# Score products of two maxima and two exponentials issued together out of four row strips, in the third attention of a two-layer adaLN transformer

## What is computed

```
q = q * cos + rotate_half(q) * sin
k = k * cos + rotate_half(k) * sin
scale = HEAD_DIM ** (-0.5)                      # HEAD_DIM = 8, 16 heads
attn = jnp.einsum('bhsd,bhtd->bhst', q, k) / scale
attn = jax.nn.softmax(attn, axis=-1)            # no mask
out = jnp.einsum('bhst,bhtd->bhsd', attn, v)
```

## Time and profile before

| | us |
|---|---|
| median of 3 runs | 2082.59 |
| lowest and highest of them | 2069.64, 2089.3 |
| the profiled execution, its own time | 2063.7 |
| its span, first to last instruction | 2061.9 |
| busy in the span: PE, VectorE, ScalarE, POOL | 1778.0, 1016.9, 724.5, 391.8 |

### The profile page before, as it was taken

How to read it: one execution, slowest core, us unless ns; L and a number is a source line. 1 busy time by engine, 2 the same in 40 slices (tenths; PEclk the granted TensorE clock), 3 DMA queues, 4 the chain that set the end, 5 groups by cost and what they waited for, 6 DMA issues and landing times.

```text
span 2061.9 us, 32743 instructions
## 1 busy us (share of the span) xinstructions
PE 1778.0 (86%) x10932; PEld 1140.9 (55%) x10932; DVE 1016.9 (49%) x2471; ACT 724.5 (35%) x1533; POOL 391.8 (19%) x614
## 2 busy tenths in 40 slices
PE   5899999799999989989799999689898989997480
PEld 2555555445555545555588888555555555554260
DVE  2445454244444443444588888555545555553103
ACT  1243434314343443444322222234435343442130
POOL 2112121121211211211000000112122212113305
PEclk7799999759898986899899999768879787875695
DMA  7000000100000000000000000100000000100133
GB/s 223 28 5 3 4 3 6 31 6 3 7 4 7 4 8 1 1 1 1 1 1 1 0 0 1 57 0 5 9 6 9 5 10 5 29 1 20 64 101 82
DMA packets 37286, 38.65 MB, mean 19 GB/s; under 512 B 4561, under 2 KB 30449, under 8 KB 36753
## 3 DMA queue, kind: packets, MB, share of 16 engines
q1 hardware_dynamic: 35088, 32.54, 5.4%
q0 software_dynamic: 2048, 4.20, 0.7%
HBM read 28.27 MB, written 8.45 MB: 18 GB/s over the span
## 4 chain that ended last, share of the span: by engine, by line
PE 75%; DVE 9%; POOL 6%; issue 5%; ACT 2%; another core or an unknown queue 1%; DMA 1%; DVEq 0%; SPq 0%; POOLq 0%; ACTq 0%
PE ps_out L1845 12%; PE ps_max L1781 8%; PE ps_four L1008 6%; PE ps_max L1019 6%; PE ps_four L1734 5%; PE ps_four L1813 4%; PE ps_work L1690 4%; PE ps_four L1804 3%; PE ps_max L1771 3%; PE ps_work L1695 3%; PE ps_four L1715 3%; PE ps_work L1715 3%; DVE row_max L1587 3%; PE ps_max L1075 1%; PE ps_four L1066 1%
## 5 line engine op out<-in xcount | busy, mean ns | idle before, releaser
L1587 DVE TENSOR_REDUCE row_max<-ps_max 128x3 f32<-128x384 f32 (+1 forms) x640 | 375.0, 607 | 310.6 <-PE ps_max L1781 309.0
L1430 ACT ACTIVATE attn_f<-ps_four 128x384 f32<-128x384 f32 (+1 forms) x640 | 336.9, 532 | 456.3 <-PE ps_four L1813 452.9
L1845 PE MATMUL ps_out<-attn_f,v_all 128*9 128x256 f32 (+3 forms) x2560 | 331.3, 386 | 0.1
L1813 PE MATMUL ps_four<-q_st,k_st 26*128 26x256 f32 (+3 forms) x1280 | 324.4, 336 | 0.0
L1781 PE MATMUL ps_max<-k_st,q_st 24*128 24x256 f32 (+3 forms) x1280 | 285.9, 363 | 37.9 <-DVE row_max L1587 24.5
L1781 PEld LDWEIGHTS ps_max<-k_st,q_st 24*128 24x128 f32 (+1 forms) x1280 | 175.7, 213 | 205.4 <-issue 142.5
L1813 PEld LDWEIGHTS ps_four<-q_st,k_st 26*128 26x128 f32 (+1 forms) x1280 | 209.9, 203 | 34.5 <-issue 26.0
L1845 PEld LDWEIGHTS ps_out<-attn_f,v_all 128*9 128x9 f32 (+1 forms) x2560 | 103.4, 95 | 148.7 <-issue 51.8
L1771 PE MATMUL ps_max<-masks,ident_bf 128*128 128x384 bf16 x384 | 130.4, 369 | 36.5 <-DVE row_max L1587 31.4
L1019 PEld LDWEIGHTS ps_max<-wd,o_both 128*128 128x128 f32 x1024 | 134.7, 193 | 18.4 <-DVE o_both L910 7.9
L1019 PE MATMUL ps_max<-wd,o_both 128*128 128x128 f32 x1024 | 136.7, 277 | 5.8 <-DVE o_both L910 5.8
(11 more groups left out here) (235 smaller groups left out, 2518.9 us busy)
## 6 DMA issues: line engine op xcount, KB each, us to landing
wd<-in_L_ffn_W SPq DMA_DIRECT2D x16, 256.0 KB, 2.8
gates_all<-in_select SPq DMA_DIRECT2D x3, 1024.0 KB, 6.9
mod<-mod_dram SPq DMA_DIRECT2D x16, 192.0 KB, 3.1
x_all<-in_L_attn_x SPq DMA_DIRECT2D x8, 256.0 KB, 6.7
slots_dram<-attn_f SPq DMA_DIRECT2D x8, 256.0 KB, 5.4
mod<-mod_dram SPq DMA_DIRECT2D x16, 128.0 KB, 3.0
gates_all<-mod_dram SPq DMA_DIRECT2D x2, 1024.0 KB, 9.6
h_tok<-slots_dram SPq DMA_DIRECT2D x8, 256.0 KB, 3.0
```

The source lines that it names most:

```text
L1430: nc.scalar.activation(probs[:, h % 4, 0:w], ps_exp[:, h % 3, 0:w], ACT.Exp, scale=c.scale).then_inc(exp_done, 1)
L1587: nc.vector.tensor_reduce(row_max[:, r2, 0:blocks, h], src, AX_X, ALU.max).then_inc(max_done, 1)
L1813: ins = nc.tensor.matmul(bank[:, k * S:(k + 1) * S - first], k_st[rows, r, g, k * P:(k + 1) * P], q_st[rows, r, g, first:S], start=not c.c ...
L1845: last = nc.tensor.matmul(ps_out[base:base + c.hd + 1, at + first:at + S], v_tok[c.index][:, r, kb, h // (c.heads // c.kv), :], probs[:, h ...
```

## The change

It touches only the third attention (`c.causal` is false). `early(c)` is 14 there, so the 16 maxima are spread over 14 slots (slots 0 and 7 get two, the others up to 13 one), and `max_order` picks them by pairs of slots. `scores` is replaced: at an even slot h one issue holds up to two maxima of the slots h and h + 1 and both exponentials, h and h + 1, in four different strips; at the odd slot only a third maximum, where there is one (slots 1 and 7), is issued by itself. The waits of an issue stand in front of all of it: for the later of the two maxima, and for the later exponential's bank. All the named pieces, the values and the orders of VectorE, ScalarE and POOL within a slot stay as they are; VectorE's maxima move to the slots of the new table.

```diff
--- before.py
+++ after.py
@@ -457,12 +457,17 @@
 
             return (c.index - 1) * NB + b
 
+        def early(c):
+
+            return (3 if c.causal else 4) * c.heads // 4 - (0 if c.causal else 2)
+
         def max_order(c):
 
-            early, left, found = 3 * c.heads // 4, list(range(c.heads)), []
-            for h in range(early):
-                taken = {h % c.per_group}
-                for _ in range(len([i for i in range(c.heads) if i * early // c.heads == h])):
+            span = 1 if c.causal else 2
+            left, found = list(range(c.heads)), []
+            for first in range(0, early(c), span):
+                taken = {h % c.per_group for h in range(first, first + span)}
+                for _ in range(len([i for i in range(c.heads) if first <= i * early(c) // c.heads < first + span])):
                     best = min(left, key=lambda k: (k % c.per_group in taken, k))
                     taken.add(best % c.per_group)
                     left.remove(best)
@@ -473,11 +478,10 @@
 
 
             names = order(c)
-            early = 3 * c.heads // 4
             table = [([], [], []) for _ in range(c.heads)]
             if with_next:
                 for i, h in enumerate(max_order(c)):
-                    table[i * early // c.heads][0].append((i, h))
+                    table[i * early(c) // c.heads][0].append((i, h))
             for j, name in enumerate(names):
                 at = 2 + j * (2 * c.heads - 2) // len(names)
                 if j < 3:
@@ -1762,7 +1766,7 @@
 
             def max_free(c, b, i):
 
-                if i == 0:
+                if i < 2:
                     pe.wait_ge(sel_out, 4 * n_of(c, b) + 4)
                 at_least(pe, max_done, HEADS_BEFORE[c.index] + b * c.heads + i - 1)
 
@@ -1829,6 +1833,28 @@
                     exp_scores(c, r, h, k)
                     for i, head in max_heads[1:]:
                         max_scores(c, (r + 1) % RING, i, head, k)
+
+            def four_scores(c, b, r, h, max_heads):
+
+                if max_heads:
+                    max_free(c, b + 1, max_heads[-1][0])
+                exp_free(c, b, h + (h > 0))
+                for k in range(BLK):
+                    for i, head in max_heads:
+                        max_scores(c, (r + 1) % RING, i, head, k)
+                    exp_scores(c, r, h, k)
+                    exp_scores(c, r, h + 1, k)
+
+            def two_slots(c, b, r, h, table):
+
+                max_heads = table[h - h % 2][0] + table[h - h % 2 + 1][0]
+                if h % 2 == 0:
+                    four_scores(c, b, r, h, max_heads[0:2])
+                else:
+                    for i, head in max_heads[2:]:
+                        max_free(c, b + 1, i)
+                        for k in range(BLK):
+                            max_scores(c, (r + 1) % RING, i, head, k)
 
             def pair_values(c, b, r, p):
 
@@ -1930,8 +1956,12 @@
                 n = n_of(c, b)
                 steps = tracked({bank_of(c, "place0"): (place_done, 2 * n + 1),
                                  bank_of(c, "place1"): (place_done, 2 * n + 2)})
-                for h, (max_heads, before, behind) in enumerate(slots(c, *flags(b))):
-                    scores(c, b, r, h, max_heads)
+                table = slots(c, *flags(b))
+                for h, (max_heads, before, behind) in enumerate(table):
+                    if c.causal:
+                        scores(c, b, r, h, max_heads)
+                    else:
+                        two_slots(c, b, r, h, table)
                     walk(c, b, r, *steps, before)
                     if h == 1 and flags(b)[0]:
                         pair_values(c, b - 1, (r - 1) % RING, c.pairs - 1)
```

## The result

Four runs of the changed kernel took 2000.13 to 2009.37 us, median 2005.47, against 2082.11 for the kernel before: ratio 0.9636, 95% interval 0.9584 to 0.9688. Six more runs of it later gave 1978.91 to 2022.73 with a ratio of 0.9716 (0.9646 to 0.9787). Over all ten the median is 2008.3. The change is faster, by 77 us in the first set and 62 in the second, where 36.7 were forecast.

What follows compares the result with a forecast made beforehand. PE was taken as the bound, but not alone: it idles 3.3 us per block, mostly in score issues waiting for VectorE's reductions. Fifteen periods at 2.35 (35.3 us) plus 1.4 make 36.7, from 2082.6 to 2046 us, range 2015 to 2085.

Steps and rivals of the forecast that it cites:

- Four strips cost what three do: A joint score issue in four strips takes 0.43 us on PE, as three strips did; upper bound 0.86.
- Start of the block: Slots 0 to 3: slot 3's own issue and wait go, combine starts earlier; 0.60 us gained, 0.72 at halved clock.
- Slots 6 to 15: Fewer issues save 1.96 us, waits grow by 0.86 to 1.97; net gain 1.10 us per block.
- A block at held clock: One block at full clock gains 0.60 + 0.43 + 1.10 = 2.13 us.
- the 2.35: Gain in us taken per block, between 2.13 and the 2.54 of blocks halved from combine to slot 5.
- The clock stays as it is: Third attention's block periods: granted clock still 0.80 to 0.83 after the change.
- The last block: Exponentials only: two issues of 0.72 go before the rank product at half clock, 1.4 us gained.
- The sum: Fifteen periods give 35.3 us, with the last block 36.7 in total; 2046 us forecast.
- the fourth strip: Rival, 0.09: it doesn't run beside the others, a joint issue costs 0.86 us; gain 13 us, time 2069.
- the wall: Rival, 0.13: VectorE's late reductions turn saved issues in slots 6 to 15 into waits; gain 18 us, time 2065.
- The second fall: Rival, 0.16: clock falls again late in the block, from `rows` on (2095) or around slots 7 and 10 (2130).
- Shorter blocks might also lose less to the clock: Side remark on the third attention's blocks, reaching down to 2015 us.

Runs made afterwards that it cites:

- second pair of profiles: Kernel before and changed kernel profiled again without edit; 506.18 and 439.98 us in the third attention's 15 periods, medians 2071.80 (one run) and 2012.45 us.
- a_split: Changed kernel's new table of maxima, but each slot issues its own maximum and exponential as before the change; 2069.13 us, ratio 0.9977.
- s_fill: Changed kernel issuing slot by slot, with unread matmuls in the pauses at slot 1 (three) and before `ht` (four); 2062.65 us.
- the filler: Four unread matmuls before `ht` in the kernel before: 2035.64 us; six in the changed kernel's three pauses at the block's head: 1967.70 us.
- its control: Kernel before with the same four unread matmuls in front of the router's product `rlog`, where PE has no pause; 2088.87 us, ratio 1.0092.
- a_pause: Changed kernel, but the joint issue of slots 2 and 3 also waits for `h_tok`, leaving one pause before it; 2027.18 us, ratio 0.9723.
- j_not23: Changed kernel with slots 2 and 3 issued slot by slot, all others jointly; 2033.52 us.

## Why the prediction was wrong, point by point

- *Four strips cost what three do*: right, 0.43 us. Nothing is added for the fourth strip. The Trainium skill (TensorE: Matmul & The Clock Gate, Part 3) has a speedup of 3.07 for four row tiles, measured there with 512 columns, which makes an estimate of 0.56 for an issue; the trace has 0.43, and decides.
- *Start of the block*: right in kind, 0.76 us instead of 0.60. One reading was wrong. I had slot 1 wait for a reduction in both kernels; before, the timeline has it wait for ScalarE's exponential, and with exponential 1 moved into the joint issue the wait shrinks from 0.86 to 0.78. The row of the kernel before:

```profile
1560.90 0.38 PE L1781 MATMUL ps_max<-k_st,q_st 24*128 24x256 f32 x1 [0.86 <-ACT attn_f L1430]
```

- *Slots 6 to 15*: 1559.38 to 1574.46 is 15.08 against 16.48, a gain of 1.40 instead of 1.10. The waits sum to 1.69 instead of 1.97, and the two placements, now neighbours, overlap by 0.09 each.
- *A block at held clock*: 2.13 was forecast, 2.7 measured (28.89 to 26.18). The term was undersized; the start of the block and slots 6 to 15 explain 0.46 of the 0.58. Against the 2.35 that went into the sum it is 5 us over fifteen periods.
- *The clock stays as it is*: this is the step that failed. I wrote "the granted clock in the periods still 0.80 to 0.83" and carried the loss over as a constant, only scaling the issues inside it. The runs showed in its place that half-clock time fell, from 181 and 192 us to 144 and 123. In both kernels the clock falls 3 to 6 us into most blocks; what is shorter is the stretch until it is back. Before, 11 of 15 such stretches take 10.2 or 13.7 us, after, 13 of 15 take 6.8 or 10.2. One of each, first of the kernel before, then of the kernel after:

```profile
1595.83:1609.48 13.65, 13.58 (x57) 8.71 (x58) 4.83 (x10) 3.11 (x6) 2.13 (x3) 0.50 0.01 2
```

```profile
1578.14:1588.38 10.24, 9.63 (x48) 6.62 (x46) 4.32 (x10) 2.78 (x6) 0.16 (x1) 0.50 0.00 1
```

  What a us of it costs follows from periods of one kernel: 26.45 at 1.00 and 29.33 at 0.88 (7.0 us at half clock), 0.41 us each. Some 37 to 69 us less make 15 to 28 us, an estimate from these rows.
- *The last block*: forecast 1.4, from the start to the rank product. Windows of the kernel before and, below it, after:

```profile
1862.02:1877.83 15.81, 15.46 (x76) 7.52 (x73) 6.08 (x20) 5.82 (x11) 0.92 (x2) 0.61 0.01 2
```

```profile
1818.92:1829.94 11.02, 9.77 (x76) 5.17 (x70) 4.85 (x14) 5.24 (x11) 0.00 (x0) 0.93 0.01 2
```

  4.8 us, again the clock, 0.61 to 0.93. In the second pair of profiles it is 7.0 us (18.03 at 0.50 to 11.02 at 0.93).
- *The sum*: 15 x 2.7 = 41, clock 15 to 28, last block 5 to 7: 61 to 76 us. The two pairs of profiles differ by 57 and 73 us in the 15 periods and the last block, which fits. The medians of all runs of this study are 2076.8 and 2008.3, 68.5 apart. Of the 32 us beyond the forecast, the clock that I held constant is the larger part.
- *The rivals*: the fourth strip was free; the reductions were not the wall. The second fall is real as a mechanism (a_split, s_fill), but the changed kernel has it only in its last full block. I asked what new pauses could cost the clock and priced that. What fewer issues and shorter pauses could give back got one sentence, "Shorter blocks might also lose less to the clock", and no term in the sum. The earlier trace rows had material for it: 5.56 us with 3.48 busy, then 0.50.

What stays open: why the changed kernel's half-clock stretches are shorter. That pauses at the head of the block bring the clock down is shown by the filler and its control. That the broken pause before `ht` is what the change gains by is not: a_pause points to it within the spread, and j_not23, in which that pause is whole, still gained 11 us over its steps by the medians.

## What to carry to other kernels

Where the clock is below 1.00 in a stage, a schedule forecast from busy times and waits is half of a forecast: ask for each pause that a change shortens, breaks up or moves what it does to the clock, and give both signs a price. To separate the two, hold the clock: put matmuls that nobody reads into the pauses of both versions and compare full-clock periods. And such filler can be worth as much as the change that it was meant to measure. Try each pause at the head of the loop body by itself: in the changed kernel the first one paid and the one before `ht` gave nothing, in the kernel before the one before `ht` paid more.

## What the runs showed of the hardware that I had not expected

- 0.65 us of unread matmuls in one pause of 0.78 raised the granted clock of the third attention from 0.84 to 0.95 and took 34 us off the time; the same kind of filler in a place without a pause, in the kernel before, cost 18.
- The clock fell to 1.2 GHz behind pauses that were all short: 0.78, 0.45 and 0.61 within 4.3 us, in most blocks of the changed kernel.
- A TensorE without pauses isn't by that at full clock: from 1595.83 to 1609.48 in the kernel before it was busy 13.58 of 13.65 us, at 0.50 all the while.
- Four score products in two strips take 0.68 us and in four strips 0.43; two products in one strip take 0.67.
- The changed kernel differs from run to run by 2.2% (1979 to 2023), and the second attention, which is the same in all kernels here, takes from 519 to 549 us between profiles.
